# Four-layer perceiver: key parts of two layers stored once each, and a key stack loaded in 48- and 16-row pieces with a copy by GpSimd

## What is computed

```python
# layer 1
q = (hidden_states @ Wq.T + bq) * scaling        # 128 x 256
k = key_value_states @ Wk.T + bk                 # 12544 x 256
v = key_value_states @ Wv.T + bv
...                                              # split into 16 heads of 16
scores = jnp.einsum('bhtd,bhsd->bhts', q, k) + bias    # bias: 16 x 128 x 12544, float32
probs = jax.nn.softmax(scores, axis=-1)
attn = jnp.einsum('bhts,bhsd->bhtd', probs, v)
# layer 3
scores = jnp.einsum('bnlh,bnph->bnlp', qm, km) / np.sqrt(HEAD_DIM).astype(np.float32)
scores = jnp.where(mask, scores, MASK_FILL)
```

## Time and profile before

| what | value |
|---|---|
| time, median of 3 runs | 2864.22 us (2858.88 to 2865.06) |
| profiled execution | 2865.3 us, its span 2863.6 us |
| TensorE busy | 2677.5 us (94 %), granted clock 0.972 on average |
| VectorE, ScalarE, GpSimd busy | 65 %, 52 %, 27 % |
| bytes moved by DMA | 578 MB, 202 GB/s over the span |

### The profile page before, as it was taken

The page is one execution under the profiler, slowest core; times in us unless marked ns, Lnnn a source line. Parts: engine busy times, 40 slices in busy tenths (PEclk is TensorE's granted clock), DMA queues, the critical chain, the costliest instruction groups (busy, mean ns, idle before and its releaser), DMA issues. The chain is left out here.

```text
span 2863.6 us, 68194 instructions
## 1 busy us (share of the span) xinstructions
PE 2677.5 (94%) x23989; PEld 1817.4 (63%) x23989; DVE 1872.3 (65%) x4087; ACT 1482.8 (52%) x2344; POOL 786.9 (27%) x512
## 2 busy tenths in 40 slices
PE   7999999998988899999989999999999889999889
PEld 4554555544767566666556666666666775666688
DVE  4677777676243788787737676777777428888632
ACT  2333333333241688888336666666666334665521
POOL 5554444543000000000006565656566100000000
PEclk9999999999999899999999999999999998999989
DMA  6989989898816999997722222222222394665455
GB/s 205 290 281 280 288 269 276 264 281 282 264 41 253 419 404 390 392 396 266 243 91 66 72 66 72 68 70 72 66 72 87 124 259 119 160 161 151 137 205 177
DMA packets 331569, 578.32 MB, mean 202 GB/s; under 512 B 79792, under 2 KB 265976, under 8 KB 325752
## 3 DMA queue, kind: packets, MB, share of 16 engines
q1 hardware_dynamic: 331408, 576.06, 61.0%
HBM read 394.96 MB, written 181.04 MB: 201 GB/s over the span
## 5 line engine op out<-in xcount | busy, mean ns | idle before, releaser
L2082 POOL TENSOR_TENSOR l2x_sums<-l2x_sums,all_S 128x768 f32<-128x768 f32 (+1 forms) x200 | 416.3, 2081 | 203.1 <-ACT all_S L2421 194.4
L2297 DVE TENSOR_TENSOR l2x_tops<-l2x_scores,l2x_tops 128x768 f32<-128x768 f32 (+1 forms) x208 | 224.7, 1080 | 193.7 <-PE l2x_scores L2146 181.0
L2130 PE MATMUL l2x_key_bank<-ahead_ctx,early_nat_out 128*64 128x512 f32 (+1 forms) x1488 | 318.1, 548 | 0.0
L1701 ACT ACTIVATE l3x_pT<-l3x_turned 128x896 f32<-128x896 f32 x224 | 197.5, 916 | 148.9 <-PE l3x_turned L1551 143.9
L1450 ACT ACTIVATE all_S<-all_S,l1x_negmax 128x896 f32<-128x896 f32 x224 | 233.3, 1044 | 45.0 <-DVE l1x_negmax L1386 26.7
L2316 DVE TENSOR_TENSOR all_S<-all_S,l2x_minus 128x1024 f32<-128x1024 f32 x224 | 232.4, 1079 | 16.9 <-PE l2x_minus L2179 16.9
L1293 PE MATMUL l1x_turned<-all_ident,all_S 128*128 128x128 f32 x1568 | 220.3, 281 | 11.9 <-ACT all_S L1450 10.5
L2421 ACT ACTIVATE all_S<-all_S 128x1024 f32<-128x1024 f32 x224 | 210.8, 956 | 22.5 <-DVE all_S L2316 22.5
L2161 PEld LDWEIGHTS l2x_out<-all_S,l2x_values 128*64 128x64 f32 x3136 | 179.6, 138 | 61.8 <-issue 60.7
L2416 ACT COPY all_S<-l2x_scores 128x1024 f32<-128x1024 f32 x224 | 199.9, 904 | 36.4 <-PE l2x_out L2161 35.8
L1293 PEld LDWEIGHTS l1x_turned<-all_ident,all_S 128*128 128x128 f32 x1568 | 173.9, 143 | 51.5 <-issue 39.1
(11 more groups left out here) (747 smaller groups left out, 5414.5 us busy)
## 6 DMA issues: line engine op xcount, KB each, us to landing
l1x_bias<-in_fside_Bx16xSxS_dram SPq DMA_DIRECT2D x112, 896.0 KB, 7.3
scratch_k<-prep_kparts SPq DMA_DIRECT2D x84, 672.0 KB, 6.1
l1x_k_half<-scratch_k SPq DMA_DIRECT2D x32, 1568.0 KB, 9.9
l2x_values<-scratch_v SPq DMA_DIRECT2D x112, 256.0 KB, 2.7
scratch_k<-prep_kparts SPq DMA_DIRECT2D x56, 448.0 KB, 6.7
scratch_v<-prep_st_v SPq DMA_DIRECT2D x11, 2048.0 KB, 8.4
scratch_v<-prep_st_v SPq DMA_DIRECT2D x14, 1536.0 KB, 10.9
l2x_values<-scratch_v SPq DMA_DIRECT2D x112, 192.0 KB, 2.6
```

The lines of the kernel that those rows point to most:

```text
L1701: nc.scalar.activation(pT[c % ring][:, :], turned_ps[c % 2][:, 0:GW], ACT.Exp).then_inc(exp_done, 1)
L2082: nc.gpsimd.tensor_tensor(sums[odd][:, 0:n], sums[odd][:, 0:n], in_memory(u), ALU.add).then_inc(added, 1)
L2130: last = nc.tensor.matmul(key_bank(h == 0, u)[half * VW:(half + 1) * VW, 0:n], wk_cur[h % 2][:, k, :], ahead.piece[u // 2][:, k, c:c + n], ...
L2297: nc.vector.tensor_tensor(by_halves(tops[:, :], u), by_halves(scores_ps[u % 2][:, :], u), by_halves(tops[:, :], u), ALU.max).then_inc(maxe ...
```

## The change

It has three parts.

**Stores in the preparation.** The scratch tensors of k1 and k3 now hold the three parts once (`scr.kparts[n]`, 3 x 256 x 12544) instead of 8 and 6 blocks. `store_parts` issues one DMA of 672 KB for a tile instead of three, so 4 instead of 12 for a group, 2688 KB instead of 6272 KB.

**l1x.** The order of the blocks changes to 0, 1, 2, 0, 0, 1, 2, 1 (with the query parts to match: the same eight products). One tile `k_all` of 128 x 12544 takes the place of the two halves. A head's keys now come in seven pieces of 1792 columns, each with three DMAs: 48 rows (parts 0 to 2) to rows 0-47, 16 rows (part 0) to rows 48-63, 16 rows (part 1) to rows 112-127. GpSimd copies rows 0-47 to rows 64-111 in each piece, when the piece's three DMAs have landed (`on_pool`). TensorE waits for that copy ahead of every second chunk of scores (7 waits a head, not 2). SyncE's order puts key piece i ahead of bias piece i.

**l3x.** A piece is loaded with three DMAs (48, 32 and 16 rows, from parts 0-2, 0-1 and 0) instead of one of 96 rows; the bytes are the same.

```diff
-PIECES = {"k1": (0, 1, 2, 0, 1, 2, 0, 1), "k3": (0, 1, 2, 0, 1, 0)}
-QPIECES = {"k1": (0, 0, 0, 1, 1, 1, 2, 2), "k3": (0, 0, 0, 1, 1, 2)}
+PIECES = {"k1": (0, 1, 2, 0, 0, 1, 2, 1), "k3": (0, 1, 2, 0, 1, 0)}
+QPIECES = {"k1": (0, 0, 0, 2, 1, 1, 1, 2), "k3": (0, 0, 0, 1, 1, 2)}
...
+        self.rows = ((0, 48), (48, 32), (80, 16))
...
     def load_k(self, sp, h, s, i):
         first, end = self.pieces[i]
         at = first % (SK // 2)
-        sp.dma_start(self.kt[s][i // 2][0:self.stack, at:at + end - first], self.k_dram[bass.ds(h, 1), :, first:end]
-                     .rearrange("a r s -> (a r) s")).then_inc(self.k_loaded[s][i], 16)
+        for row, n in self.rows:
+            sp.dma_start(self.kt[s][i // 2][row:row + n, at:at + end - first], self.k_dram[bass.ds(h, 1), 0:n, first:end]
+                         .rearrange("a r s -> (a r) s")).then_inc(self.k_loaded[s][i], 16)
...
                         hold(sp, held, parts_ready, g * 4 + i + 1 + 2)
-                        for at, n_parts in COPIES[n]:
-                            sp.dma_start(scr.kstack[n][at:at + n_parts, t * P:(t + 1) * P, bass.ds(g * GW, GW)]
-                                         .rearrange("a p s -> p a s"),
-                                         kparts[i % 2][:, 0:n_parts, :]).then_inc(parts_stored[i % 2], 16)
+                        sp.dma_start(scr.kparts[n][:, t * P:(t + 1) * P, bass.ds(g * GW, GW)]
+                                     .rearrange("a p s -> p a s"), kparts[i % 2][:, :, :]).then_inc(parts_stored[i % 2], 16)
...
-                        act.wait_ge(parts_stored[nk % 2], (g * 2 + nk // 2 + 1) * 16 * N_COPIES)
+                        act.wait_ge(parts_stored[nk % 2], (g * 2 + nk // 2 + 1) * 16)
...
-    def load_keys(sp, h, j, first):
+    def load_keys(sp, h, i, first):
...
-                hold(sp, held, scores_full, (h - 1) * 2 * GRP + GRP * (j + 1))
-            for dst, src in k_loads(h, j):
-                sp.dma_start(dst, src).then_inc(k_loaded[j], 16)
+                hold(sp, held, scores_full, (h - 1) * 2 * GRP + 4 * (i + 1))
+            for dst, src in k_loads(h, i):
+                sp.dma_start(dst, src).then_inc(k_loaded[i], 16)
...
         for i in range(GRP // 2):
             if k is not None:
+                load_keys(sp, k, i, first)
                 load_bias(sp, k, i, first)
-                if i == 2:
-                    load_keys(sp, k, 0, first)
-                if i == 6:
-                    load_keys(sp, k, 1, first)
...
-        if k_loads is not None and c % (GRP // 2) == 0:
-            j = c // (GRP // 2)
-            pe.wait_ge(k_loaded[j], (h + 1) * 16 * n_k)
+        if k_loads is not None and c % 2 == 0:
+            pe.wait_ge(k_copied, h * (GRP // 2) + c // 2 + 1)
...
+    def on_pool(pool):
+
+        with pool.Fori(0, heads) as h:
+            for i in range(GRP // 2):
+                hold(pool, held_by_pool, k_loaded[i], (h + 1) * 16 * n_k)
+                cols = slice(i * 2 * GW, (i + 1) * 2 * GW)
+                nc.gpsimd.tensor_copy(k_all[64:64 + PARTS * 16, cols], k_all[0:PARTS * 16, cols]).then_inc(k_copied, 1)
...
+        def k_load(h, i):
+
+            cols = slice(i * 2 * GW, (i + 1) * 2 * GW)
+            return [(k_all[row:row + n_rows, cols], k_dram[bass.ds(h, 1), at:at + n_rows, cols].rearrange("a r s -> (a r) s"))
+                    for row, at, n_rows in ((0, 0, 48), (48, 0, 16), (112, 16, 16))]
```

More of the change, by code:

```diff
@@ L438, in wait_before_chunk @@
             for s in self.parts:
-                sp.wait_ge(s, 16 * N_COPIES * (2 * GRP + 1))
+                sp.wait_ge(s, 16 * (2 * GRP + 1))
         if c == 7:
@@ L1135, with head_stream @@
 LAG = 3
-def head_stream(nc, ph, com, heads, vw, att, v_src, q=None, k_half=None, k_loads=None, bias=None, ring=R, lag=LAG,
+def head_stream(nc, ph, com, heads, vw, att, v_src, q=None, k_all=None, k_loads=None, bias=None, ring=R, lag=LAG,
                 by_vector=(1, 3, 5, 8, 10, 12), q_cur=None,
@@ L1167, in head_stream @@
     copied = {"v": S("copied_by_vector"), "s": S("copied_by_scalar")}
-    k_loaded = [S(f"k_loaded{j}") for j in range(2)]
+    k_loaded, k_copied = [S(f"k_loaded{i}") for i in range(GRP // 2)], S("k_copied")
     v_loaded = [S(f"v_loaded{j}") for j in range(2 if heads > 1 else GRP)]
-    held, held_by_vector = S("held"), S("held_by_vector")
+    held, held_by_vector, held_by_pool = S("held"), S("held_by_vector"), S("held_by_pool")
     by = ["v" if c in by_vector else "s" for c in range(GRP)]
@@ L1459, in head_stream @@
     run.on_sync, run.on_tensor, run.on_vector, run.on_scalar = on_sync, on_tensor, on_vector, on_scalar
+    run.on_pool = on_pool
     return run
@@ L1487, in head_stream_turned @@
                        "cleared", "held"))
-    N_K = 1
+    N_K = len(keys.rows)
     NB = 2 * GRP
@@ L1779, in cross_attention_16 @@
             places_ready = ph.sem("places_ready")
-        k_half = None if masked else [ph.sb(f"k_half{j}", [rows, SK // 2], BF16) for j in range(2)]
-        def k_load(tile, h, j):
-            cols = slice(j * (SK // 2), (j + 1) * (SK // 2))
-            return [(tile[0:stack, :], k_dram[bass.ds(h, 1), :, cols].rearrange("a r s -> (a r) s"))]
+        k_all = None if masked else ph.sb("k_all", [rows, SK], BF16)
+        def k_load(h, i):
+            cols = slice(i * 2 * GW, (i + 1) * 2 * GW)
+            return [(k_all[row:row + n_rows, cols], k_dram[bass.ds(h, 1), at:at + n_rows, cols].rearrange("a r s -> (a r) s"))
+                    for row, at, n_rows in ((0, 0, 48), (48, 0, 16), (112, 16, 16))]
         fside = a["fside_Bx16xSxS2_0"]
@@ L1951, in _ @@
                     nc.gpsimd.memset(q_stack[stack:stack + 3, :], 0.0).then_inc(rows_set, 1)
+                else:
+                    run.on_pool(pool)
 def l2_cross_attention(nc, com, a, scr, ahead, spare, load_next):
```

38 lines of the change are left out of this document (14 added, 24 removed).

## The result

| | time, median | lowest to highest | profiled execution, span |
|---|---|---|---|
| before, timed beside it | 2862.72 us (4 runs) | 2858.88 to 2865.06 | 2863.6 us |
| changed | 2977.18 us (4 runs) | 2963.88 to 2982.78 | 2974.0 us |

The ratio is 1.0385, with a 95 % interval of 1.0368 to 1.0402: 3.85 % or 114 us slower by the medians, 110.4 us by the spans of the two profiled executions. The four times of the changed kernel lie within 19 us, those of the kernel before within 6; in 15 later executions the kernel before scattered over 15 us too.

What follows compares the result with a forecast made beforehand. TensorE, busy 94 % of the span, was taken to bound the kernel, with the DMA engines close behind in l1x. 2865.3 - 17 + 52 + 28 + 3 = 2931.3, with the median 1.1 lower: 2930 us, range 2848 to 3005.

Steps and rivals of the forecast that it cites:

- preparation: Preparation: fewer key stores end the waits of ScalarE's casts and so TensorE's wait; -17 us, bounds 0 and -28.
- l1x: l1x: narrow key transfers make the DMA engines the bound, 30.0 us a head against 26.47; +52 us, bounds -5.5 and +138.
- l3x's start: Before l3x's first scores: the keys loaded ahead, 3.6 MB, take a fifth longer; +3 us, between 0 and +7.
- l3x, per head: l3x: key loads without slack, split in three, cost +2.0 us in each of 14 heads; +28 us, bounds -2.6 and +41.
- 219 GB/s for 48 rows: l1x: rate taken for 48-row key transfers from 96-row ones; 1.20 MB a head in 5.5 us.
- 110 for all: Rival, narrow transfers slower: all keys at 110 GB/s, 35.4 us a head, l1x +138, time 3033 us; slower still had 0.14.
- likeliest case: DMA-bound l1x at 28 to 34 us a head, l3x between 0 and +48; 2880 to 3000 us, chance 0.56.
- the DMA engines keep up: Rival: l1x stays TensorE-bound and gains 5.5 us, l3x loses 9 to 31; time 2851 or 2873 us, chance 0.24.
- GpSimd as the bound: Rival in l1x: at 3.8 us a copy a head takes 27.2 us, +11 us, time 2868 us; chance 0.03.

Runs made afterwards that it cites:

- the last kernel: Changed kernel with l1x's keys in one 128-row transfer a piece (five stored blocks) and l3x's in one 96-row transfer; median 2838.4 us, 0.9899 of before.

## Why the prediction was right, and where it was off

It forecast 2930 us in a range of 2848 to 3005, slower; measured were 2977, inside the range but 47 us above the forecast. Term by term, beside the profiled execution:

| term | forecast | measured |
|---|---|---|
| preparation | -17 | -19.8 |
| l1x | +52 | +98.3 |
| l3x's start | +3 | +4.9 from the end of l1x on |
| l3x, per head | +28 | +27.8 |
| sum | +66 | +110.4, with the rest |

**The preparation** went as worked out. The casts' waits for the key store are gone, and what comes last for the fourth cast is ScalarE's own cast before it: in a group of the changed kernel the two start at 315.74 us and take 1.94 us together, without a gap. TensorE's 17.0 us became 1.1. The table began at 60 us and so left a wait of 1.8 us out. That fewer stores help held; that it is what is stored of a k1 tile, the run with 96 and 32 rows shows.

**l1x** had the right mechanism and the wrong size. The DMA engines became the bound, with a full share, a rate of 281 GB/s (305 forecast) and 33.4 us a head (30.0 forecast). The term that failed is "219 GB/s for 48 rows": by what they add to a head they came to 112 to 120, no more than 16 rows, for which I had 110 and the runs give 130. The keys cost 16.2 us in place of 12.8, and 16 x 3.4 = 54 us covers the 46 that were missing in l1x. The 8 us between them: the sum had 16 heads and 4 us more, and the stage took 530.3 us, 4 us less than 16 heads of 33.4. Why was not followed up. The reason I gave, that fewer rows than 96 can hardly be faster, is a bound from one side; I took it as the value. The bound from the other side, 110 for all, was the nearer one. The run with 96 and 32 rows also shows that 219 GB/s belongs to l3x's own mix: beside the 128-row bias they came to 140. And the sum priced each kind by itself, as if the bias kept its 420 GB/s; in the trace its packets are slowed as well, from 272 to 405 ns.

**The figures of the Trainium skill** that the prediction set beside its sum, 104 GB/s for 16 partitions and 196 for 64 (page "SBUF — State Buffer", section "Door 1: The DMA port swizzle (why `[64,N]` ≈ `[32,N]`)"), gave 31.1 us a head by estimate, nearer to 33.4 than mine was. For 16 rows the runs agree roughly, with 130 GB/s by what they add to a head. For 64 rows they don't: 119 GB/s with 16 rows beside them. The Trainium skill's rule in the section "Can I just issue two DMAs to hit both halves?" of that page, that only one transfer over all 128 partitions reaches all 16 ports, is what the last kernel follows for l1x. The trace bears out that it pays: 402 GB/s in l1x, where 96 and 32 rows in two transfers left 261.

**l3x** came out at the size forecast, and in part by luck. +2.0 us a head was forecast from a third piece without slack. TensorE's waits from 2400 to 2850 us:

```profile
PE l3x_last L1540 <- DMA keys_k<-scratch_k: 21.2, 11, 2.5
PE l3x_scores L1540 <- DMA keys_k<-scratch_fill: 6.7, 1, 6.7
```

The first is the mechanism forecast, but in 11 heads, and 18.6 us above the 2.6 of the earlier trace rows, not 28. The stage from its first score to its last, before and after, tells where the rest is:

```profile
2361.00:2683.00 322.00, 307.53 (x4770) 208.56 (x4771) 274.33 (x608) 186.35 (x210) 0.00 (x0) 0.96 0.57 146
```

```profile
2445.00:2794.50 349.50, 317.84 (x4774) 214.46 (x4774) 277.03 (x608) 186.97 (x210) 0.00 (x0) 0.93 0.65 134
```

TensorE's idle time grew by 17.2 us, and its busy time by 10.3 us with the same products, at a granted clock of 0.93 in place of 0.96. With l3x's keys in one transfer again, the waits and the busy time are both back, the busy time at 307.4 us and a clock of 0.96. A slower clock beside the waits was in no term of the sum.

The second wait above is the price for the keys loaded ahead, 6.7 us in place of 2.3: +4.4, where +3 was forecast. The 3.6 MB behind that +3 are not in the rows; the six key pieces loaded ahead are 4.8 MB.

**The ends of the likeliest case**, 2880 to 3000, do not follow from its terms: with +20 to +117 and 0 to +48 beside -17 they are 2867 to 3012. The range that was stated is hardly touched by it.

**The rivals.** That the DMA engines keep up is refuted by the share and by the length of a head. GpSimd as the bound is refuted by its 1.68 us a copy (1.8 forecast) and by the run with twice the copies. The five further waits of TensorE cost next to nothing of their own, 3.2 us in 3 waits for the copy. What I had not put into the sum is VectorE held by GpSimd at the start of l1x; as the DMA engines set the end of the stage, it has no effect on the time that these runs show.

## What to carry to other kernels

A load that fetches fewer bytes can be slower: 80 rows of a tile in 48- and 16-row transfers added 16.2 us to a head, all 128 rows in one transfer no more than 9.3. The cost does not stay with the narrow transfers: the wide ones queued beside them slow down too. Where a tile holds the same data several times, look for an access pattern on the source that repeats it (shifted windows over a few more stored blocks), with the large dimension outside (64 outer entries here, where 2 failed), before copying on chip. And where the price of an operation is missing from a trace, bounds are not enough if the nearest row bounds it from one side only: a rate taken from transfers among their own kind did not hold beside others.

## What the runs showed of the hardware

- What key transfers add to a head beside the 128-row bias, as their bytes over the length of a head less 17.2 us: 16 rows 130 GB/s, 48 rows 112 to 120, 64 with 16 rows 119, 96 with 32 rows 140; 128 rows at least 346 (3.21 MB in the 9.27 us that a head of 26.47 leaves). Among themselves, 96-row transfers moved 219. In these mixes, from 16 to 96 rows, the figure hardly depends on the rows, and hardly on the number of transfers (6, 14, 21 or 35 a head).
- Narrow transfers spread among wide ones slow these too: a 7168-byte row of the bias took 272 ns before, 405 ns beside 48- and 16-row key transfers, 445 ns beside 96- and 32-row ones, and 274 ns beside 128-row ones of the same piece size.
- Two outer entries in a source of 128 rows left the DMA share at 0.38 and the rate at 124 GB/s; 64 outer entries over the same bytes gave 1.01 and 402 GB/s. That a transfer is dealt to the engines by its outermost dimension fits both; the deal itself was not looked at.
- Why narrow transfers fill the engines' time without moving bytes is open: the runs with all of their key rows in narrow transfers show a share of 0.99 to 1.03, a low rate and longer packets, none shows what the packets wait for.
- A VectorE instruction that met a copy by GpSimd lasted until that copy was over: one bfloat16 copy of 256 columns 1702 ns (219 in the median), one float32 scaling 1254 ns (294), and both were back when GpSimd was held. VectorE's bias addition stayed at a median of 620 ns with and without GpSimd's copies.
- With TensorE waiting more in l3x, its granted clock was 0.93 in place of 0.96 and the same products kept it busy for 317.8 us in place of 307.5.
